# Two attention layers on one core: head pairs taken two at a time, with scores and transposes on half-height tiles of TensorE

## The reference

```
n = layer_norm(x);  x = x + attention(n, n)          # "self", 20 heads of 64
n = layer_norm(x);  x = x + attention(n, context)    # "cross", 20 heads of 64
x = x + geglu_ff(layer_norm(x))                      # 160 -> 2*640 -> 160, gelu
# second layer: 20 heads of 8, context split into 73 text rows and 4 image rows
probs_t = softmax(q @ k_t * s);  text = probs_t @ v_t
sem = cosine(probs_t @ context_t, context_ip)
probs_ip = softmax(q @ k_ip * s + 0.5 * sem) * mask
out = (text + probs_ip @ v_ip) @ W_out + b + x
```

## Time and profile before

| | |
|---|---|
| median of 3 runs | 3804.21 us (3803.1 to 3806.92) |
| span of the profiled execution (first to last instruction) | 3799.1 us, so the runs are 4.0 to 7.8 us above it |
| PE busy | 95% |
| PEld busy | 88% |
| ACT busy | 68% |
| DVE busy | 67% |
| POOL busy | 36% |

### The profile page before, as it was taken

The page is one execution under the profiler, slowest core; times in us unless marked ns, Lnnn a source line. Parts: engine busy times, 40 slices in busy tenths (PEclk is TensorE's granted clock), DMA queues, the critical chain, the costliest instruction groups (busy, mean ns, idle before and its releaser), DMA issues.

```text
span 3799.1 us, 88944 instructions
## 1 busy us (share of the span) xinstructions
PE 3608.9 (95%) x29708; PEld 3328.8 (88%) x29708; DVE 2547.7 (67%) x8159; ACT 2592.4 (68%) x8021; POOL 1352.4 (36%) x1658
## 2 busy tenths in 40 slices
PE   6999999999999999999999999999999999999997
PEld 5888989889898898988989899898988989889897
DVE  6667666676766666676676766767667676666766
ACT  6667676766767667676676766767676676766764
POOL 2233343333433334333333433334333343333433
PEclk9999999999999999999999999999999999999998
DMA  6522314223142321413223132231422313232130
GB/s 169 163 64 75 103 44 119 60 85 91 41 122 58 96 77 51 123 47 106 70 60 117 45 112 65 76 103 44 121 57 87 90 41 121 58 96 77 53 93 18
DMA packets 210716, 313.38 MB, mean 82 GB/s; under 512 B 31232, under 2 KB 167520, under 8 KB 210272
## 3 DMA queue, kind: packets, MB, share of 16 engines
q1 hardware_dynamic: 209984, 307.53, 27.6%
q10 hardware_dynamic: 288, 0.16, 0.0%
HBM read 267.97 MB, written 14.42 MB: 74 GB/s over the span
## 4 chain that ended last, share of the span: by engine, by line
PE 60%; DVE 17%; ACT 11%; issue 8%; POOL 4%; DMA 1%; SPq 0%; ACTq 0%; DVEq 0%; POOLq 0%
PE PS L818 8%; PE PT L840 6%; PE PV L854 6%; PE PW L798 5%; PE PG L659 5%; ACT SE L989 4%; PE PG L651 4%; PE PG L634 4%; PE PV L864 3%; DVE sums L1233 3%; PE PG L637 3%; PE PG L635 3%; PE PG L636 3%; POOL SE L1404 3%; PE PG L742 2%
## 5 line engine op out<-in xcount | busy, mean ns | idle before, releaser
L1404 POOL TENSOR_TENSOR SE<-SE,rs 128x512 f32<-128x512 f32 (+1 forms) x640 | 557.6, 871 | 1761.8 <-DVE rs L1238 1761.8
L989 ACT ACTIVATE SE<-PS,mx 128x128 f32<-128x128 f32 (+2 forms) x3840 | 982.6, 346 | 240.7 <-DVE qq L1262 128.5
L975 ACT ACTIVATE PTs<-PT 128x512 f32<-128x512 f32 (+2 forms) x960 | 575.4, 599 | 87.1 <-PE PT L840 67.9
L840 PE MATMUL PT<-ident,SE 128*128 128x128 f32 (+2 forms) x3840 | 582.0, 274 | 36.4 <-POOL SE L1404 34.6
L1233 DVE TENSOR_REDUCE sums<-SE 128x4 f32<-128x512 f32 (+1 forms) x640 | 367.0, 573 | 337.8 <-ACT SE L989 336.9
L1222 DVE TENSOR_REDUCE mx<-PS 128x4 f32<-128x512 f32 (+2 forms) x960 | 504.4, 525 | 72.1 <-PE PS L818 58.7
L840 PEld LDWEIGHTS PT<-ident,SE 128*128 128x128 f32 (+2 forms) x3840 | 465.5, 144 | 64.5 <-POOL SE L1404 49.0
L1396 POOL TENSOR_TENSOR n<-qq,p_half 128x4 f32<-128x4 f32 x320 | 345.3, 1079 | 490.2 <-DVE qq L1262 490.1
L798 PE MATMUL PW<-w_o,OTs 128*128 128x160 f32 x2560 | 415.3, 299 | 1.1 <-ACT OTs L967 1.1
L818 PE MATMUL PS<-qk 128*128 128x256 f32 x1280 | 348.5, 395 | 47.6 <-ACT qk L915 47.6
L912 ACT ACTIVATE qk<-PG 128x256 f32<-128x256 f32 x640 | 252.9, 395 | 190.1 <-PE PG L637 186.5
(11 more groups left out here) (207 smaller groups left out, 7828.5 us busy)
## 6 DMA issues: line engine op xcount, KB each, us to landing
q_slice<-q_split SPq DMA_DIRECT2D x630, 192.0 KB, 2.4
vc_slice<-vc_split SPq DMA_DIRECT2D x155, 512.0 KB, 3.6
kc_slice<-kc_split SPq DMA_DIRECT2D x150, 256.0 KB, 2.7
q1st<-q_hi SPq DMA_DIRECT2D x320, 32.0 KB, 1.9
k1st<-k_hi SPq DMA_DIRECT2D x160, 38.5 KB, 1.9
xres<-in_x_dram SPq DMA_DIRECT2D x32, 160.0 KB, 2.3
q1st<-q_lo SPq DMA_DIRECT2D x160, 32.0 KB, 1.9
out_dram<-x SPq DMA_DIRECT2D x64, 80.0 KB, 1.6
```

The source lines that it names most:

```text
L840: last = tr(PT[0:J, 128 * i:128 * i + 128], SE[:, place % 4, J * i:J * i + J], ident[:, :])
L975: a_(PTs[0:J, place % 3, :], PT[0:J, :], ACT.Copy).then_inc(S["pts_done"], 1)
L989: last = a_(SE[:, place % 4, J * i:J * i + J], PS[place % 2][:, step * i:step * i + J], ACT.Exp, bias=mx[:, place % 2, i:i + 1])
L1404: gp.tensor_tensor(e, e, rs[:, n % 2, :].unsqueeze(2).to_broadcast([128, 4, J]), ALU.mult)\
```

## The change

The slots are kept in number (60 to a group), but three of them make a beat, and a beat holds one duo (two l0 units, that is two head pairs) and one l1 unit, regularly. All lists for the first and the last group go, but one; so does `keep_busy`. The l1 units of a group are in beats 21 to 40 after the group's first, so that the last 20 hold no l0 unit.

- `scores(g, d)` does a duo: eight products of 64 rows, alternately on the upper and the lower 64 rows of the array, each row half into a bank of its own (PS is now 2 banks for one duo). The keys carry no zeros any more.
- `probs_transposed(g, d)`: 16 transposes of 64 rows in place of 8 of 128, alternately on the two row halves, each half into its own bank of PT (2 banks).
- `probs_v(g, d)`: as before, but a duo into the one bank PV. The l1 units transpose into PT bank 0, have their scores in PT bank 1, and their products in PV.
- ACT: one copy of 512 columns for `qk` (three instructions before in self attention), one for OTs of a duo, one of 1024 for the transposes of a duo; `kc` copies go to DVE alone. The query scale is folded into the split weights.
- Norms, context scale, ff, and the x loads have new slots: `norm_out` comes two slots after the statistics and `xT` three. `ff` is in slots 51, 52, 53, 53, 54 and 66, 67, 68, 68, 69 in place of five in one slot, twice.
- `cT` and `x1` have two copies; `gv` and `PTs1` lie in memory freed after the weights are split; `gv` is set to one by POOL in slot 47.

```diff
-    L1_SLOT = [6, 7, 9, 10, 11, 13, 14, 15, 17, 18, 22, 26, 27, 29, 33, 36, 38, 45, 49, 53]
-    NORM_SLOT = {(0, 0): -12, (0, 1): -2, (1, 0): 25, (1, 1): 40, (2, 0): 52, (2, 1): 65, (3, 0): 60, (3, 1): 71}
-    FF_SLOT = [56, 56, 56, 56, 56, 68, 68, 68, 68, 68]
+    BEATS = 20
+    STEP = 3 * BEATS
+    NORM_SLOT = {(0, 0): -16, (0, 1): -1, (1, 0): 17, (1, 1): 32, (2, 0): 47, (2, 1): 62, (3, 0): 56, (3, 1): 71}
+    FF_SLOT = [51, 52, 53, 53, 54, 66, 67, 68, 68, 69]
+    DOWN_SLOT = [55, 70]
...
+                def scores(g, d):
+                    q = DUOS * g + d
+                    J, h = K0[2 * d // U0], 2 * d // NP % 2
+                    if q > 0:
+                        pe.wait_ge(S["exp_done"], 2 * q)
+                    for n in (2 * d, 2 * d + 1):
...
                         for b in range(HB):
-                            last = mm(ps[:, 2 * J * b:2 * J * b + 2 * J], qk[:, n % 2, 0, 128 * b:128 * b + 128],
-                                      keys[:, :, J * b:J * b + J], start=True, stop=True)
+                            for e in range(2):
+                                rows, at = slice(DH * e, DH * e + DH), J * (2 * (n % 2) + b)
+                                last = mm(PS[:, e, at:at + J], qk[rows, n % 2, 0, 128 * b:128 * b + 128],
+                                          keys[rows, J * b:J * b + J], start=True, stop=True)
...
+                def probs_transposed(g, d):
+                    q, J = DUOS * g + d, K0[2 * d // U0]
+                    if q > 0:
+                        pe.wait_ge(S["pts_done"], q)
+                    if scored1[0]:
+                        pe.wait_ge(S["exp1_done"], scored1[0])
...
+                            for r in range(2):
+                                rows, at = slice(64 * r, 64 * r + 64), 64 * (4 * (n % 2) + i)
+                                last = tr(PT[0:J, r, at:at + 64], SE[rows, n % 4, J * i:J * i + J], ident[rows, rows])
...
# TensorE, in each slot t = 3 * beat + part
+                    if part == 0:
+                        if duo_at(beat + 1):
+                            scores(*duo_at(beat + 1))
+                        if duo_at(beat):
+                            probs_transposed(*duo_at(beat))
+                        if duo_at(beat - 1):
+                            probs_v(*duo_at(beat - 1))
                     for name in qk_at(t):
                         job(name)
...
+                    if part == 1 and l1_at(beat - 1):
+                        probs_transposed1(*l1_at(beat - 1), turned)
+                    if part == 1 and l1_at(beat):
+                        scores1(*l1_at(beat), turned)
+                    if part == 2 and duo_at(beat - 1):
+                        g, d = duo_at(beat - 1)
+                        wo(g, 2 * d)
+                        wo(g, 2 * d + 1)
+                    if part == 2 and l1_at(beat - 1):
+                        probs_v1(*l1_at(beat - 1), multiplied)
...
# ScalarE, in each slot
+                    if sub == 0 and l1_at(beat - 1):
+                        exp1(*l1_at(beat - 1))
+                    if sub == 0 and duo_at(beat):
+                        pt_out(*duo_at(beat))
+                    if sub < 2 and duo_at(beat + 1):
+                        g, d = duo_at(beat + 1)
+                        exp(g, 2 * d + sub)
                     for name in qk_at(t):
                         job(name)
-                    if t - PT_LAG in UNIT_AT:
-                        pt_out(UNIT_AT[t - PT_LAG])
+                    if sub == 0 and duo_at(beat - 1):
+                        ot_out(*duo_at(beat - 1))
+                    if sub == 1 and l1_at(beat - 1):
+                        pt1_out(*l1_at(beat - 1))
```

More of the change, by code:

```diff
@@ L416, in xattn_program @@
             + [(STEP * g + K1_SLOT[r], ("k1", g, r)) for g in range(GROUPS) for r in range(2)]
             + [(STEP * g + VIP_SLOT, ("vip", g, 0)) for g in range(GROUPS)]
-            + [(ctx1_slot(g, b), ("ctx1", g, b)) for g in range(GROUPS) for b in range(GB)])
+            + [(STEP * g + CTX1_SLOT[b], ("ctx1", g, b)) for g in range(GROUPS) for b in range(GB)])
         def qk_at(t):
-            if l0_at(t + 2) is None:
+            duo = duo_at(t // 3 + 2)
+            if t % 3 == 2 or duo is None:
@@ new lines, in probs_v @@
+                def probs_v(g, d):
+                    q, J = DUOS * g + d, K0[2 * d // U0]
+                    pe.wait_ge(S["pts_done"], q + 1)
+                    pe.wait_ge(S["v_done"], q + 1)
+                    if q > 0:
+                        pe.wait_ge(S["ots_done"], q)
+                    if product1[0]:
+                        pe.wait_ge(S["on_done"], product1[0])
+                    for u in range(2):
+                        for b in range(HB):
+                            for e in range(2):
+                                at = 128 * (2 * e + b)
+                                last = mm(PV[DH * e:DH * e + DH, HT * u + 128 * b:HT * u + 128 * b + 128],
+                                          v_sb[0:J, d % 2, b, 2 * u + e, :], PTs[0:J, q % 2, u, at:at + 128],
+                                          start=True, stop=True)
+                    last.then_inc(S["pv_done"], 1)
@@ new lines, in probs_v1 @@
+                def probs_v1(g, k, multiplied):
+                    b, w, j = k // W1, k % W1, l1_count(g, k)
+                    pe.wait_ge(S["pts1_done"], j)
+                    if multiplied:
+                        pe.wait_ge(S["ots_done"], multiplied)
+                    if j > 1:
+                        pe.wait_ge(S["on_done"], j - 1)
+                    if w == 0:
+                        pe.wait_ge(S["gv_done"], NTH[("ctx1", g, b)])
+                        pe.wait_ge(S["gram_done"], NTH[("ctx1", g, b)])
+                    for i in range(4):
+                        off = D1 * (i % 2)
+                        last = mm(PV[:, GV * i + off:GV * i + off + GS + D1], PTs1[0:TT, 128 * i:128 * i + 128],
+                                  gv[:, b % 2, 2 * w + i // 2, off:off + GS + D1], start=True, stop=True)
+                    last.then_inc(S["pv1_done"], 1)
+                    product1[0] = j
@@ L988, in exp, with pt1_out @@
                     for i in range(4):
-                        last = a_(SE[:, place % 4, J * i:J * i + J], PS[place % 2][:, step * i:step * i + J], ACT.Exp,
-                                  bias=mx[:, place % 2, i:i + 1])
+                        e, b = divmod(i, 2)
+                        at = 2 * e2 + b
+                        last = a_(SE[:, n % 4, J * i:J * i + J], PS[:, e, J * at:J * at + J], ACT.Exp,
+                                  bias=mx[:, q % 2, 4 * e + at:4 * e + at + 1])
                     last.then_inc(S["exp_done"], 1)
+                def pt1_out(g, k):
+                    j = l1_count(g, k)
+                    act.wait_ge(S["pt1_done"], j)
+                    if j > 1:
+                        act.wait_ge(S["pv1_done"], j - 1)
+                    a_(PTs1[0:TT, :], PT[0:TT, 0, :], ACT.Copy).then_inc(S["pts1_done"], 1)
@@ new lines, in exp1 @@
+                def exp1(g, k):
+                    j = l1_count(g, k)
+                    act.wait_ge(S["mx1_done"], j)
+                    act.wait_ge(S["sip_in"], j)
+                    if j > 2:
+                        act.wait_ge(S["qq_done"], j - 2)
+                    for i in range(4):
+                        last = a_(SE1[:, j % 2, TT * i:TT * i + TT], PT[:, 1, T * i:T * i + TT], ACT.Exp,
+                                  bias=mx1[:, j % 2, i:i + 1])
+                    last.then_inc(S["exp1_done"], 1)
@@ L997, in context_squares @@
                         act.wait_ge(S["c_dve"], HB * (2 * g + h))
+                    if g > 0:
+                        for w in range(W1):
+                            act.wait_ge(S[f"k1_in{w}"], 16 * 3 * g)
                     for b in range(HB):
```

504 lines of the change are left out of this document (219 added, 285 removed).

## The result

The changed kernel takes 4316.8 us, median of four runs (4314.51 to 4322.96), against 3805.57 before: 1.1347 times as long (95% interval 1.1331 to 1.1363), where 3755 was forecast. The profiled execution has a span of 4321.2 us against 3799.1, so 522 us are to be found.

A forecast was written before the change was run, and what follows sets the result against it. PE's own instruction stream was taken as the bound. Per group -13.5 stream, -8.3 old waits, +18.5 new waits gave -3.3; 3799.1 - 15 x 3.3 - 8 + 8 = 3750, plus 5 to median 3755 us; range 3560 to 3930.

The forecast's parts named there:

- The wider spacing of the norm (three slots): Norm's steps in the new slots: covered by the beat's other work; up to 4 x 2 us a group without it.
- a plain beat: Beat without extra jobs: just closes, ACT's chain 6.3 against PE's 6.2 us (self); forecast fails if not 7.7 to 8.5.
- PE's stream: PE's work per group falls 13.5 us: scores save 10.1, transposes 4.4, changes of tile shape cost 1.
- Weight loads in turn (third rival): Scores' row halves load one after the other: 4030 us, to 4300 if transposes do so too; chance 0.12.
- Waits: PE's waits per group: 18.5 us new, in ff, `kc` and `xT` beats, and the 8.3 of old ones go.
- the four ff beats: Gelus between exponentials: 12 table loads a group, 192 in all; `exp1` and transposes wait, 13 us a group.
- The four `kc` beats: Five `kc` beats a group, five jobs on two banks PG: 0.5 us of waiting each, 2.5 in all.
- the ten beats with `xT` or `cT`: Only two beats, with `xT`, `q1`, `ctx1` and the image part, were priced: 1.5 us each, 3 a group.
- The clock: After the last block, without `keep_busy`: may stay at its lower level longer than mean 0.88 shows; part of the end's +8.
- Second rival (the loop through ACT decides): Handovers through ACT cost more, each 0.1 us per beat 32; at 0.4, 3885; idle over 25 a group; chance 0.25.
- The end and the first group: End: l1 units alone at 3.1 us a beat, 62 for 20, +8 us overall; first group: PE's saving only, -8.

The follow-up runs named there:

- norm_out_early: Changed kernel with the norm's last step and the context scale moved on DVE from the end of the slot to its head; 4109.23 us, ratio 1.0797.
- best_late: combo_norm_stats with the last norm of each half group one slot earlier (55 and 70); 3661.17 us, ratio 0.9619.
- scores_one_half: Changed kernel with both heads' score products on the upper 64 rows, same number of products, another output; 4486.16 us, ratio 1.1768.
- combo: Changed kernel with each half group's ff jobs in one slot and the l1 exponentials and maximum earlier; 4087.45 us, ratio 1.0739.
- fill_at_norms: Changed kernel with 12 products without use on PE ahead of each `xT` and `cT` job from the second group on; 4283.46 us, ratio 1.126.
- combo_norm_stats: combo plus the edit of norm_out_early, and the norm's statistics on DVE behind the next duo's maximum; 3759.39 us, ratio 0.9875.
- exp1_mx1_early: Changed kernel with l1 exponentials in the last slot of their own beat on ACT and their maximum a slot earlier on DVE; 4242.65 us, ratio 1.1158.
- combo_fill: combo plus products without use ahead of `xT` and `cT` jobs, ahead of each duo's transposes and in the end; 4196.32 us, ratio 1.1032.

## Why the prediction was wrong

**The sentence that failed** is "The wider spacing of the norm (three slots) is covered by the beat's other work, and would cost up to 4 x 2 us a group without it". I had counted the spacing on PE and the work on DVE, but not where norm and scale stand in DVE's order. There they are inside the loop scores, maximum, exponentials, sums, transposes, next scores. That order alone is worth 208 us (norm_out_early), and 210 + 118 with the other waits away. Ten beats of a group hold an `xT` or `cT`. Eight of them took 10.9 to 12.9 us (means over 14 groups), where I had a plain beat at 7.7 to 8.5; the one that is plain took 8.6, just outside. The two in which the last norm's `xT` fell between `qk` jobs took 16.7 and 15.4, in best_late 12.6 each.

**PE's stream**: right. -12.5 us a group against -13.5. Its terms: scores, 16 x 0.057 and 16 x 0.056 against 1.72 and 1.03, save 8.0 + 1.4 = 9.4 (forecast 10.1); transposes at 0.031 to 0.035 save some 7 (forecast 4.4). With most waits gone and the clock at 1.00 it shows in the time, 14.7 us less: best_late's group has 220.3 - 11.3 = 209.0 us of stream, the kernel before 232.1 - 8.4 = 223.7.

**Weight loads in turn (third rival)**: refuted. The rule of the Trainium skill ("TensorE: Matmul & The Clock Gate", section LDWEIGHTS) that half-height loads cost whole ones fits scores_one_half, 0.116 apiece on one half; on two halves the products come at half of that, so it doesn't bite here.

**Waits**: 18.5 us new and 8.3 gone were forecast, net +10.2 a group; it was +29.3. The kinds that I named are there: the four ff beats took 15.9, 17.4, 16.2 and 17.2 us in the kernel after and 15.4, 13.9, 14.9 and 16.6 with gelus together, 190 loads against my 192; the transposes do wait for `exp1`. Together they are 229 us of the time (combo), 15 a group, where I had 13 for the ff beats. The four `kc` beats without an `xT` waited 0.5 to 0.8 us each, near my 0.5. What I had almost at nothing is the ten beats with `xT` or `cT`: 3 us for two of them, and 22 measured.

**The clock**: forecast only for the end. It came with short waits alone, in 26 us of each group, and that costs at most 13 us a group, 195 us over 15 groups, by the account above; the one run that gave most of it back (fill_at_norms) gained 33. The Trainium skill (same page, section "A second HAM failure mode: psum-queue depth-cycling") tells of a kernel in which PE's short pauses between groups of matmuls make the clock go back and forth; this trace agrees, with no wait above 2.0 us between 700 and 3400 us and a mean of 0.95.

**Second rival (the loop through ACT decides)**: its sign, and its mark of over 25 us idle per group, came true. Its mechanism did so in part: the loop does decide, but the lateness enters on DVE, not by small handovers, and it is 13.1 - 11.4 = 1.7 us a beat where 0.4 was its worst case. So I held the loop to be nearly closed on ACT (6.3 against 6.2 us) and never added up DVE's chain in it.

**The end and the first group**: +8 forecast, +49 measured; 3.1 us an l1 unit forecast, 6.4 measured. A unit alone takes 3.5, near my chain; what I had left out is what else comes in between, above all the image part. The first group was to gain 8 and lost 33. It has the same norms: in combo_norm_stats its last block starts 7 us later than before and no longer 33.

**Sums**: forecast error per group 19 (waits) + 13 (clock, its upper bound) + 1 (stream) = 33 us, which are the 29.8 measured and the 3.3 forecast the other way.

That gains don't add (combo 229 for 66 and 74; with norm_out_early 439 for 66, 74 and 208) has three reasons that the runs show: the waits lie on one loop, so a delay taken away at one place comes back at the next while another remains; exp1_mx1_early alone adds 60 table loads that combo doesn't have; and the clock rises as the waits go (0.95, 0.97, 0.99, 1.00). Beyond the ff beats' part, how much of the surplus is each one's wasn't separated.

## What to carry to other kernels

When work is put into longer, coarser beats, write down for each engine what stands between two steps of the loop that feeds the bound engine, side work too; a side chain (norm, scale, statistics) belongs behind the loop's next step and ahead of the one that would wait, and moving three such steps was worth 328 us here (210 + 118), more than the 262 of the row halves. A saving on the bound engine is real only if its order stays fed, so measure it in a version whose waits are gone before judging it: the same row halves were worth 79 and 183 us there, while the change as a whole came out 511 us slower. Don't price a wait by its row; take it away and see where it comes back.

## What was unexpected of the hardware

- Products on the two row halves ran side by side even when four of one half stood together in the program: 16 in 1.18 us in place of 1.12, transposes 0.77 in place of 0.71 or 0.77; on one half alone 2.01.
- 16 transposes of 64 rows on two halves are 0.031 us apart, well below the 0.054 that was the shortest distance in the rows of the kernel before.
- The granted clock fell to its lower level in the midst of a stream that was busy for 86% of the time and, from 700 to 3400 us, never waited over 2.0 us at once; by the account above that cost at most 195 us over 15 groups. Products without use bring it back, but gained only where they lay in idle time (-33 us in fill_at_norms, +109 in combo_fill against combo).
